# A two-layer language model tower on one core: TensorE multiplies a constant matrix in its waits of the expert stage, and GpSimd's additions for a result are spread over four slots

## The chip, the cores and the metric

The kernel runs on one core of one Trainium2 chip. The core has TensorE (PE, matrix multiply, with its weight loads in a row of their own, PEld), VectorE (DVE), ScalarE (ACT), GpSimd (POOL) and SyncE (SP, which issues DMAs). The metric is the device time of one execution in microseconds (us), lower is better. It is compared as the median of several executions.

## The reference, cut to what matters

16384 tokens of 128 channels go through a token table and four residual layers:

```python
h = tok_table[x]                              # (64, 256, 128)
h = h + linear_attention(layernorm(h))        # first layer
h = h + expert_choice_ffn(layernorm(h))       # 32 experts, each picks its 512 best tokens
h = h + causal_attention(layernorm(h))        # 8 heads of 128, 64 sequences of 256 tokens
h = h + top2_ffn(layernorm(h))                # 8 experts, each token uses 2

# expert_choice_ffn, for expert e: rows idx = its 512 tokens with the highest router probability
up  = tokens[idx] @ W_up[e // 4] + b_up[e // 4]          # 128 -> 341
out = silu(up) @ W_down[e] + b_down[e]                   # 341 -> 128
y[idx] += prob[idx, e] * out
```

All of it is float32.

## The kernel before

The kernel is one program with semaphores placed by hand. The order of instructions on each engine is the order in which the code issues them; no scheduler moves anything. Four stages follow each other: the first layer with the router, the search for each expert's threshold, the **expert stage** (32 experts one after the other), and a long **slot stage** that does the causal attention of 512 sequence-heads in 512 slots (`u` counts them) and, two portions behind, the top-2 feed-forward network.

**The expert stage.** For expert `e` GpSimd issues four indirect DMAs that gather its 4 x 128 token rows into `rows4` (`take(e)`, L836), and later four that scatter the updated rows back (`give(e)`, L845). Its order is `take(e + 1)`, `give(e)`, `take(e + 2)`, `give(e + 1)` and so on. TensorE does per expert, in this order: `rows(e + 2)` (L2000, four matmuls that number the tokens of a later expert), `turn_rows(e)` (L2012, four transposes of the gathered rows into bank 0, behind the wait for the gathers of `e`), then, when ScalarE has copied the transposed rows to `xeT` (L1047), the up product (L2024, three column blocks, with the two small `bases(e + 3)` matmuls L1993 between the second and the third), then, when ScalarE has applied silu (L1059), the down product (L2037, 12 matmuls of fp32, 24 in the profile's count). VectorE counts and places the tokens of later experts, and weighs each down product into `rows4` (L1485), which releases `give(e)`. The gather of `e` must have been issued and landed before `turn_rows(e)`; `give(e)` needs the first L1485 of `e`.

A helper `keep_busy` of the stage before (L1944) already multiplies the constant `slot16` (fp16, 128 x 512) into an unused bank; nothing reads the product. The expert stage has no such multiplications.

**The slot stage.** In slot `u` each engine does a fixed list of things for heads `u`, `u - 1`, ... and, for the feed-forward part, for a unit of 128 token rows. SP loads units; TensorE, ScalarE and VectorE compute one; VectorE ends it with `unit_out` (L1742), and GpSimd scatters it in `give_unit` (L881). In four slots of eight GpSimd also does one `scatter` of normalised rows (L866), and at the first slot of eight `residual` (L875, two additions). From slot 256 on VectorE normalises the softmax (L1567, L1570), and once a slot copies a transposed head out of PSUM (L1577).

When a portion's units are all scattered, results are put together: a table `RESULT_AT` says that in slot `r` SP loads the two expert rows (`zx`, tile name `junk`) and the residual (`h3x`, `pc`) of 512 tokens. GpSimd adds the two rows in slot `r + 2` (`add_rows`, L890, four additions of 128 x 128, behind the wait `z_in` for the loads) and the residual in slot `r + 3` (`add_residual`, L896, four more), and SP stores the result. GpSimd does so for 22 results, those of the first two portions, from slot 386 to 495; consecutive results of a portion are four slots apart. The later ten results are done by VectorE.

Of the kernel before, what the change touches and what calls it, by code (L numbers as in the profile page):

```python
# [12 lines left out]
ALU = mybir.AluOpType  # L13
# [3 lines left out]
P = 128  # L17
C = 128
NTOK = 64 * 256
NT = NTOK // P  # L20
TG = 4
# [67 lines left out]
def lm_tower(nc, x, L0_tok_weight, L0_attn_Wqkv, L0_attn_temperature, L0_attn_Wproj, L0_attn_bproj,  # L89
# [3 lines left out]
    with ExitStack() as ctx:  # L93
# [6 lines left out]
        bank = [ctx.enter_context(nc.psum_tensor(f"bank{n}", [P, 512], F32)) for n in range(8)]  # L100
# [79 lines left out]
        slot16 = sb("slot16", [P, CAP], F16)  # L180
# [140 lines left out]
        zx = junk[:].bitcast(F32).rearrange("p (q j c) -> p q j c", q=2, j=TG)  # L321
# [163 lines left out]
        res_step = sem("res_step")  # L485
# [10 lines left out]
        def gated(i):  # L496
            return 0 <= i < NG
# [237 lines left out]
        def _(pool):  # L735
# [146 lines left out]
                    ap=xu_at(t)[:, C + 1:XW].bitcast(U32), axis=0), in_=yu[:, t % YR], in_offset=None,  # L882
                    bounds_check=2 * NTOK - 1, oob_is_err=False).then_inc(z_out[t % YR], 16)

            def add_rows(c):
                pool.wait_ge(z_in[c % 2], 32 * (c // 2 + 1))
                if c >= 2:
                    pool.wait_ge(out_done[c % 2], 16 * (c // 2))
                for j in range(TG):
                    ins = pool.tensor_tensor(res[:, c % 2, j], zx[:, c % 2, j, 0:C], zx[:, c % 2, j, C:2 * C], ALU.add)  # L890
                ins.then_inc(res_step, 1)

            def add_residual(c):
                pool.wait_ge(res_step, c + 1)
                for j in range(TG):
                    ins = pool.tensor_tensor(res[:, c % 2, j], res[:, c % 2, j], h3x[:, c % 2, j], ALU.add)  # L896
                ins.then_inc(res_ready, 1)

            def normalise(u, h):
                pool.wait_ge(rinv_ready, u + 1)  # L900
                pool.tensor_scalar(pr[:, u % PRN, 0:P], pr[:, u % PRN, 0:P], rinv[:, h % 4, 0:1], None, ALU.mult)  # L901
                pool.tensor_scalar(pr[:, u % PRN, P:3 * P], pr[:, u % PRN, P:3 * P], rinv[:, h % 4, 1:2], None, ALU.mult)\  # L902
                    .then_inc(pr_ready_pool, 1)

            for u in range(NI * 2 * H1):
                n, h = u // H1, u % H1
                i, p = n // 2, n % 2
                if h == 0 and n < NB:
                    residual(n)
                if 0 <= u - N_LAG < POOL_NORM:  # L910
                    normalise(u - N_LAG, (h - N_LAG) % H1)
                if gated(i - 2) and i <= NG and 1 <= h <= TG:
                    if u - 1 <= U:
                        pool.wait_ge(exp_ready, u - 1)
                    scatter(i - 2, p, h - 1)
                if i == NG + 1 and p == 0:
                    scatter(NG - 1, h // TG, h % TG)
                if u - 2 in STEP_AT and STEPS[STEP_AT[u - 2]][2] is not None:
                    give_unit(STEPS[STEP_AT[u - 2]][2])
                if u - 2 in RESULT_AT and u < U:  # L920
                    add_rows(RESULT_AT[u - 2])
                if u - 3 in RESULT_AT and u <= U:
                    add_residual(RESULT_AT[u - 3])
            for q in range(YR):
                pool.wait_ge(z_out[q], given(UNIT0[NK], q))

# [897 lines left out]
        def _(pe):  # L1824
# [179 lines left out]
            for e in range(3):  # L2004
                bases(e)
                if e < 2:
                    rows(e)

            def turn_rows(e):
                pe.wait_ge(xe_in[e % 2], 64 * (e // 2 + 1))  # L2010
                for c in range(TG):
                    ins = pe.transpose(bank[0][:, c * P:(c + 1) * P], rows4[:, e % NTAB, c, 0:C], ident[:])  # L2012
                ins.then_inc(xeT_mm, 1)

            def serve(v, last):
                for q in range(4):
                    e, p = 4 * v + q, q % 2
                    if not (last and q >= 2):
                        rows(e + 2)
                    turn_rows(e)  # L2020
                    pe.wait_ge(xeT_ready, e + 1)
                    pe.wait_ge(wup_in[p], 16 * (2 * v + q // 2 + 1))
                    for k in range(3):
                        pe.matmul(bank[1 + k][0:FCH[k], :], wup[:, p, k * P:k * P + FCH[k]], xeT[:], start=True, stop=True)\  # L2024
                            .then_inc(up_mm, 1)
                        if k == 1 and not (last and q >= 1):
                            bases(e + 3)
                    pe.wait_ge(ac_ready, 3 * e + 3)
                    pe.wait_ge(wdn_in[p], 48 * (2 * v + q // 2 + 1))
                    for c in range(TG):  # L2030
                        if c == 1 and not (last and q >= 1):
                            pe.wait_ge(oneh_ready, e + 4)
                        if TG * e + c >= 2:
                            pe.wait_ge(ye_ready, TG * e + c - 1)
                        for k in range(3):
                            m = FCH[k] + (k == 2)
                            ins = pe.matmul(down_at(c), ac[0:m, k, c * P:(c + 1) * P], wdn[0:m, p, k],  # L2037
                                            start=(k == 0), stop=(k == 2))
                        ins.then_inc(dn_mm, 1)
# [190 lines left out]
```

## Time and profile before

| | |
|---|---|
| median of 3 runs | 2584.89 us (2581.69 to 2586.2) |
| the profiled execution, its own time | 2591.4 us |
| span of the profiled execution | 2589.7 us |
| busy: PE, DVE, ACT, POOL | 2264.2, 1896.1, 1686.8, 1473.5 us |
| mean granted TensorE clock | 0.955 of full speed |

The span is what the records cover; the own time is what the same execution took by the clock that the comparisons use, 1.7 us more. The profiled execution is 6.5 us above the median of the others. Every time at which something starts is counted from the span's start.

### The profile page before, as it was taken

The numbers are of one execution on the slowest core, as the hardware profiler recorded it, in microseconds if no ns is written. First come the engines' busy times: TensorE is split into PE (matmuls) and PEld (weight loads), VectorE is DVE, ScalarE is ACT, GpSimd is POOL, SyncE is SP. The second block draws the span as 40 slices with busy tenths as digits, with TensorE's granted clock in tenths as the row PEclk, the third lists the DMA queues.
The fourth block names the chain that finished last, engine by engine and source line by source line (L and its number), as shares of the span: only waits on it lengthen the run. The fifth ranks groups of instructions, "written<-read, shape, count | busy, mean of one in ns | idle before, by whom it ended". The sixth has DMA issues, their size and how long they took to land.

```text
span 2589.7 us, 59542 instructions
## 1 busy us (share of the span) xinstructions
PE 2264.2 (87%) x16671; PEld 1982.4 (77%) x16687; DVE 1896.1 (73%) x8436; ACT 1686.8 (65%) x5272; POOL 1473.5 (57%) x1870
## 2 busy tenths in 40 slices
PE   4988978576776899999999999999999999999954
PEld 4877756344443788988888899999998888988854
DVE  4877756656663688888888887887788888888622
ACT  3777744122222777777777788888887777777643
POOL 6444200467766578788888864444444665366553
PEclk9999989789888999999999999999999999999987
DMA  2666630244444611111111146566546776476687
GB/s 73 212 229 205 222 121 1 83 138 142 140 135 131 138 42 42 46 45 49 47 44 46 43 135 171 161 163 172 165 134 187 222 217 198 128 227 196 174 254 241
DMA packets 343687, 357.42 MB, mean 138 GB/s; under 512 B 36491, under 2 KB 285931, under 8 KB 343360
## 3 DMA queue, kind: packets, MB, share of 16 engines
q1 hardware_dynamic: 305856, 265.69, 35.9%
q0 software_dynamic: 34048, 80.03, 9.5%
q10 hardware_dynamic: 3456, 7.89, 1.0%
q8 instruction: 138, 2.26, 0.4%
q14 instruction: 189, 1.55, 0.2%
HBM read 211.02 MB, written 136.67 MB: 134 GB/s over the span
## 4 chain that ended last, share of the span: by engine, by line
PE 54%; DVE 22%; DMA 7%; issue 7%; POOL 4%; ACT 3%; SPq 2%; ACTq 0%; DVEq 0%; POOLq 0%
PE bank L2068 6%; PE bank L2158 6%; PE bank L2144 5%; PE bank L2079 4%; PE bank L2024 4%; PE bank L2111 4%; PE bank L2119 3%; PE bank L2067 3%; PE bank L2091 3%; PE bank L2093 3%; PE bank L2092 3%; PE bank L2037 3%; DVE pr_place L1577 2%; DMA rows<-table,idx 2%; DVE nmax L1557 2%
## 5 line engine op out<-in xcount | busy, mean ns | idle before, releaser
L881 POOL DMA_INDIRECT zbuf<-pc,kb x248 | 250.4, 1010 | 272.8 <-DVE pc L1742 221.9
L866 POOL DMA_INDIRECT spread_rows<-kb,pos x256 | 256.1, 1000 | 171.3 <-DVE pc L1742 81.0
L1081 ACT ACTIVATE pr_place<-bank,nmax 128x128 f32<-128x128 f32 x512 | 188.5, 368 | 223.6 <-DVE nmax L1557 223.5
L2068 PE MATMUL bank<-xT,gT 128*128 128x256 f32 x1024 | 307.4, 382 | 0.0
L1577 DVE COPY pr_place<-bank 128x384 f32<-128x384 f32 x512 | 280.6, 548 | 9.2 <-PE bank L2079 7.8
L2158 PE MATMUL bank<-wvo_part,x_part 128*128 128x512 f32 x768 | 269.3, 459 | 0.0
L2079 PE MATMUL bank<-ident,pr_place 128*128 128x128 f32 x1536 | 252.3, 273 | 17.2 <-DVE pr_place L1577 17.0
L1556 DVE TENSOR_REDUCE nmax<-bank 128x1 f32<-128x128 f32 x512 | 142.9, 279 | 169.1 <-PE bank L2068 167.2
L1091 ACT ACTIVATE bank<-causal 128x384 f32<-128x384 f32 x512 | 253.4, 495 | 19.5 <-PE bank L2202 3.3
L2079 PEld LDWEIGHTS bank<-ident,pr_place 128*128 128x128 f32 x1536 | 195.4, 140 | 87.1 <-DVE pr_place L1570 22.1
L2144 PE MATMUL bank<-x_part,wqk_part 128*128 128x256 f32 x1536 | 245.6, 296 | 1.2 <-DVE x_part L1684 1.2
L1083 ACT ACTIVATE pr_place<-bank,nmax 128x256 f32<-128x256 f32 x512 | 242.4, 473 | 0.0
L902 POOL TENSOR_SCALAR pr_place<-pr_place,rinv 128x256 f32<-128x256 f32 x256 | 239.5, 936 | 0.0
L901 POOL TENSOR_SCALAR pr_place<-pr_place,rinv 128x128 f32<-128x128 f32 x256 | 155.4, 607 | 134.4 <-DVE rinv L1563 129.2
L836 POOL DMA_INDIRECT rows<-table,idx x128 | 124.0, 968 | 163.6 <-DVE idx L1470 125.2
L1154 ACT ACTIVATE vo_place<-bank 128x512 f32<-128x512 f32 x256 | 153.1, 598 | 95.8 <-PE bank L2158 95.0
L2091 PE MATMUL bank<-vo_place,pr_place 128*128 128x128 f32 x1024 | 200.6, 278 | 16.8 <-DVE pr_place L1577 15.4
L2067 PE MATMUL bank<-xT,gT 128*128 128x128 f32 x1024 | 203.7, 280 | 10.5 <-ACT gT L1151 10.4
L1557 DVE TENSOR_REDUCE nmax<-bank 128x1 f32<-128x256 f32 x512 | 211.2, 412 | 0.0
L2144 PEld LDWEIGHTS bank<-x_part,wqk_part 128*128 128x128 f32 x1536 | 199.8, 190 | 1.8 <-DVE x_part L1684 1.6
L2093 PE MATMUL bank<-vo_place,pr_place 128*128 128x128 f32 x1024 | 198.6, 276 | 0.0
L2092 PE MATMUL bank<-vo_place,pr_place 128*128 128x128 f32 x1024 | 198.5, 276 | 0.0
(338 smaller groups left out, 6472.9 us busy)
## 6 DMA issues: line engine op xcount, KB each, us to landing
pa<-bundle SPq DMA_DIRECT2D x198, 321.0 KB
table<-rows SPq DMA_DIRECT2D x96, 576.0 KB, 7.0
rows<-table SPq DMA_DIRECT2D x192, 128.0 KB
wu_more<-bundle SPq DMA_DIRECT2D x66, 321.0 KB
junk<-zbuf SPq DMA_DIRECT2D x32, 512.0 KB
kb<-spread_rows SPq DMA_DIRECT2D x248, 65.0 KB
h3buf<-h SPq DMA_DIRECT2D x64, 128.0 KB
kb<-kb SPq DMA_DIRECT2D x32, 256.0 KB
```

Source lines behind the costliest of these rows:

```text
L866: pool.indirect_dma_start(out=spread_rows, out_offset=bass.IndirectOffsetOnAxis(ap=pos[:, k, j:j + 1], axis=0), in_=xr4s[g % 2][:, k, j], ...
L1091: act.activation(bank[SBANK[u % 2]][:, 0:3 * P], causal[:], ACT.Copy).then_inc(mask_set, 1)
L1557: dve.tensor_reduce(nmax[:, h % 4, 1:2], s2[:, P:3 * P], AX.X, ALU.max, negate=True).then_inc(max_ready, 1)
L1577: dve.tensor_copy(prT[:, h % 2], t_bank(u)[:, 0:3 * P]).then_inc(prT_ready, 1)
L2067: pe.matmul(s2[:, 0:P], g[:, 0:P], xT3[:, p, 0:P], start=False, stop=True, skip_group_check=True)
L2068: pe.matmul(s2[:, P:3 * P], g[:, P:2 * P], xT3[:, p], start=False, stop=True, skip_group_check=True)\
L2079: ins = pe.transpose(t_bank(u)[:, k * P:(k + 1) * P], pr[:, u % PRN, k * P:(k + 1) * P], ident[:])
L2091: pe.matmul(o[:, 0:P], prT[:, h % 2, 0:P], v0, start=(h == 0), stop=False, skip_group_check=True)
L2092: pe.matmul(o[:, P:2 * P], prT[:, h % 2, P:2 * P], v0, start=False, stop=False, skip_group_check=True)
L2093: pe.matmul(o[:, P:2 * P], prT[:, h % 2, 2 * P:3 * P], v1, start=False, stop=(h == H1 - 1), skip_group_check=True).then_inc(head_mm, 1)
L2144: ins = pe.matmul(bank[GBANK][:, k * 2 * P:(k + 1) * 2 * P], wqk_part[a][:, h + k], x_part[b][:, p], start=(m == 0), stop=(m == 2))
L2158: ins = pe.matmul(bank[VBANK][:, :], x_part[b][:, p, (h % 2) * P:(h % 2 + 1) * P], wvo_part[a][:, 4 * (h // 2):4 * (h // 2) + 4], start=(m ...
```

## The change

In the expert stage TensorE gets eight more matmuls for each expert: six of `slot16` into bank 0 ahead of the wait for the gathered rows, and two into bank 3 behind the transposes. Both banks are written again by the expert's own work before anything is read from them. In the slot stage GpSimd's eight additions for a result are no longer four in slot `r + 2` and four in slot `r + 3`, but two in each of the slots `r + 2` to `r + 5`: one ahead of the slot's `scatter` and `give_unit`, and one behind them.

```diff
-            def add_rows(c):
-                pool.wait_ge(z_in[c % 2], 32 * (c // 2 + 1))
-                if c >= 2:
-                    pool.wait_ge(out_done[c % 2], 16 * (c // 2))
-                for j in range(TG):
-                    ins = pool.tensor_tensor(res[:, c % 2, j], zx[:, c % 2, j, 0:C], zx[:, c % 2, j, C:2 * C], ALU.add)
-                ins.then_inc(res_step, 1)
+            def add_rows(c, j):
+                if j == 0:
+                    pool.wait_ge(z_in[c % 2], 32 * (c // 2 + 1))
+                    if c >= 2:
+                        pool.wait_ge(out_done[c % 2], 16 * (c // 2))
+                ins = pool.tensor_tensor(res[:, c % 2, j], zx[:, c % 2, j, 0:C], zx[:, c % 2, j, C:2 * C], ALU.add)
+                if j == TG - 1:
+                    ins.then_inc(res_step, 1)
...
+            def adding(u, later):
+                for d in range(2):
+                    if u - 2 - d in RESULT_AT and u - d < U:
+                        add_rows(RESULT_AT[u - 2 - d], 2 * d + later)
+                    if u - 4 - d in RESULT_AT and u - 2 - d < U:
+                        add_residual(RESULT_AT[u - 4 - d], 2 * d + later)
...
+                adding(u, 0)
                 if gated(i - 2) and i <= NG and 1 <= h <= TG:
...
-                if u - 2 in RESULT_AT and u < U:
-                    add_rows(RESULT_AT[u - 2])
-                if u - 3 in RESULT_AT and u <= U:
-                    add_residual(RESULT_AT[u - 3])
+                adding(u, 1)
...
+            def stay_warm(b, times):
+                for _ in range(times):
+                    pe.matmul(bank[b][:, :], slot16[:, 0:P], slot16[:], start=True, stop=True)
+
             def turn_rows(e):
+                stay_warm(0, 6)
                 pe.wait_ge(xe_in[e % 2], 64 * (e // 2 + 1))
...
                     turn_rows(e)
+                    stay_warm(3, 2)
                     pe.wait_ge(xeT_ready, e + 1)
```

(`add_residual` is cut in the same way as `add_rows`.)

TensorE in the expert stage, one expert, before; `oneh` and `tab` belong to the numbering of a later expert, `rows4` holds the gathered rows:

```order
L2000 MATMUL bank5<-tab,oneh 128x129 [waits oneh_ready]
L2000 MATMUL bank5<-tab,oneh 128x129
L2000 MATMUL bank6<-tab,oneh 128x129 x2
L2012 MATMUL bank0<-ident,rows4 128x128 [waits xe_in0]
L2012 MATMUL bank0<-ident,rows4 128x128 x3
L2024 MATMUL bank1<-xeT,wup 128x512 [waits wup_in0,xeT_ready]
L2024 MATMUL bank2<-xeT,wup 128x512
L1993 MATMUL bank7<-cum,before 128x2 [waits cum_ready]
L2024 MATMUL bank3<-xeT,wup 85x512
```

The same place on TensorE after (the lines are those of the changed file: L2012 has become L2024, L2024 has become L2037):

```order
L2007 MATMUL bank5<-tab,oneh 128x129 [waits oneh_ready]
L2007 MATMUL bank5<-tab,oneh 128x129
L2007 MATMUL bank6<-tab,oneh 128x129 x2
L2018 MATMUL bank0<-slot16 128x512 x6
L2024 MATMUL bank0<-ident,rows4 128x128 [waits xe_in1]
L2024 MATMUL bank0<-ident,rows4 128x128 x3
L2018 MATMUL bank3<-slot16 128x512 x2
L2037 MATMUL bank1<-xeT,wup 128x512 [waits wup_in1,xeT_ready]
L2037 MATMUL bank2<-xeT,wup 128x512
L2000 MATMUL bank7<-cum,before 128x2 [waits cum_ready]
L2037 MATMUL bank3<-xeT,wup 85x512
```

Six matmuls stand between the numbering and the wait `xe_in`, and two between the transposes and the wait `xeT_ready`; nothing else has moved.

GpSimd in the slot stage, slots `r + 2` and `r + 3` of the result with `out_done0`, before:

```order
L866 DMA spread_rows<-kb,pos 141312x130 [waits exp_ready]
L881 DMA zbuf<-pc,kb 32768x128 [waits yu_ready]
L890 TENSOR_TENSOR pc<-junk 128x128 [waits out_done0,z_in0]
L890 TENSOR_TENSOR pc<-junk 128x128 x3
L866 DMA spread_rows<-kb,pos 141312x130 [waits exp_ready]
L881 DMA zbuf<-pc,kb 32768x128 [waits yu_ready]
L896 TENSOR_TENSOR pc<-pc 128x128 [waits res_step]
L896 TENSOR_TENSOR pc<-pc 128x128 x3
```

GpSimd from slot `r + 2` to slot `r + 5` of the same result, after (L897 is the old L896):

```order
L890 TENSOR_TENSOR pc<-junk 128x128 [waits out_done0,z_in0]
L866 DMA spread_rows<-kb,pos 141312x130 [waits exp_ready]
L881 DMA zbuf<-pc,kb 32768x128 [waits yu_ready]
L890 TENSOR_TENSOR pc<-junk 128x128 x2
L866 DMA spread_rows<-kb,pos 141312x130 [waits exp_ready]
L881 DMA zbuf<-pc,kb 32768x128 [waits yu_ready]
L890 TENSOR_TENSOR pc<-junk 128x128
L897 TENSOR_TENSOR pc<-pc 128x128 [waits res_step]
L866 DMA spread_rows<-kb,pos 141312x130 [waits exp_ready]
L881 DMA zbuf<-pc,kb 32768x128 [waits yu_ready]
L897 TENSOR_TENSOR pc<-pc 128x128 x2
L881 DMA zbuf<-pc,kb 32768x128 [waits yu_ready]
```

Two runs of four additions have become runs of one or two, with a scatter between them; the wait for the loads (`z_in`) has moved ahead of the scatters of slot `r + 2`, which stood in front of it.

## Rows read from the trace of the kernel before

**Rows 1.** Expert stage: us; PE, PEld, DVE, ACT, POOL busy; PEclk, DMA share, GB/s.

```profile
486.00:828.00 342.00, 249.37 (x1245) 156.86 (x1246) 195.01 (x786) 85.98 (x141) 238.16 (x245) 0.90 0.44 137
```

**Rows 2.** Timeline of GpSimd, expert stage: start, duration, [idle before, releaser].

```profile
488.82 1.01 POOL L845 DMA_INDIRECT table<-rows,idx  x1 [9.84 <-DVE rows L1485]
...
598.86 1.00 POOL L845 DMA_INDIRECT table<-rows,idx  x1 [1.50 <-DVE rows L1485]
...
609.07 1.00 POOL L845 DMA_INDIRECT table<-rows,idx  x1 [0.30 <-DVE rows L1485]
...
633.76 0.99 POOL L845 DMA_INDIRECT table<-rows,idx  x1 [2.18 <-issue]
...
641.40 0.95 POOL L836 DMA_INDIRECT rows<-table,idx  x1 [0.30 <-DVE rows L1485]
...
655.94 1.00 POOL L845 DMA_INDIRECT table<-rows,idx  x1 [3.37 <-DVE rows L1485]
...
817.59 1.00 POOL L845 DMA_INDIRECT table<-rows,idx  x1 [0.30 <-issue]
```

**Rows 3.** Timeline of TensorE, two experts in a row.

```profile
645.34 1.12 PE L2012 MATMUL bank<-ident,rows 128*128 128x128 f32 x4 [4.32 <-DMA rows<-table,idx]
647.14 3.78 PE L2024 MATMUL bank<-xeT,wup 128*128 128x512 f32 x4 [0.69 <-ACT xeT L1047]
...
653.76 3.05 PE L2037 MATMUL bank<-wdn,ac 128*128 128x128 f32 x24 [0.77 <-ACT ac L1059]
656.65 0.39 PE L2000 MATMUL bank<-tab,oneh 128*128 128x129 f16 x4
656.88 0.61 PE L2012 MATMUL bank<-ident,rows 128*128 128x128 f32 x4
658.17 1.98 PE L2024 MATMUL bank<-xeT,wup 128*128 128x512 f32 x4 [0.69 <-ACT xeT L1047]
...
662.45 3.07 PE L2037 MATMUL bank<-wdn,ac 128*128 128x128 f32 x24 [0.77 <-ACT ac L1059]
665.36 0.39 PE L2000 MATMUL bank<-tab,oneh 128*128 128x129 f16 x4
668.25 0.66 PE L2012 MATMUL bank<-ident,rows 128*128 128x128 f32 x4 [2.51 <-DMA rows<-table,idx]
```

**Rows 4.** Single microseconds of the same two experts, the columns of rows 1.

```profile
643.00:644.00 1.00, 0.00 (x0) 0.00 (x0) 0.96 (x4) 0.00 (x0) 0.69 (x2) 0.50 1.06 331
...
658.00:659.00 1.00, 0.83 (x2) 0.49 (x3) 0.97 (x8) 0.30 (x3) 0.70 (x2) 1.00 0.92 267
```

**Rows 5.** Timeline of TensorE in the threshold search: the constant multiplications there.

```profile
359.64 1.02 PE L1944 MATMUL bank<-slot 128*128 128x512 f16 x4
...
362.70 0.59 PE L1944 MATMUL bank<-slot 128*128 128x512 f16 x2
```

**Rows 6.** Line L1577 in two stretches of the slot stage: count, durations, first and last start.

```profile
L1577 DVE COPY pr_place<-bank x96: 536/547/558, 1592.0 to 1923.9; 128x384 f32<-128x384 f32 x96
L1577 DVE COPY pr_place<-bank x49: 536/545/558, 1979.7 to 2164.9; 128x384 f32<-128x384 f32 x49
```

**Rows 7.** Timeline of VectorE and GpSimd at one run of additions.

```profile
2048.96 2.89 DVE L1567 TENSOR_SCALAR pr_place<-pr_place,rinv 128x128 f32<-128x128 f32 x1
...
2049.67 1.70 POOL L896 TENSOR_TENSOR pc<-pc 128x128 f32<-128x128 f32 x4
2051.32 0.86 POOL L875 TENSOR_TENSOR hb<-hx,bo 128x128 f32<-128x128 f32 x2
```

**Rows 8.** Groups by line, VectorE, 1600 to 1900 us, then 1975 to 2165 us.

```profile
L1567 DVE TENSOR_SCALAR pr_place<-pr_place,rinv 128x128 f32<-128x128 f32 x86 | 29.1, 339 | 0.0
...
L1567 DVE TENSOR_SCALAR pr_place<-pr_place,rinv 128x128 f32<-128x128 f32 x49 | 29.3, 598 | 0.0
```

**Rows 9.** Groups by line and shape, GpSimd, 1975 to 2380 us.

```profile
L881 POOL DMA_INDIRECT zbuf<-pc,kb x100 | 101.3, 1013 | 90.0 <-DVE pc L1742 67.9 <-issue 19.3 <-DMA out_dram<-pc 2.7
...
L890 POOL TENSOR_TENSOR pc<-junk 128x128 f32<-128x128 f32 x88 | 38.2, 467 | 28.0 <-DMA pc<-h3buf 27.9
```

More of the change, by code:

```diff
@@ L883, in give_unit, with add_residual @@
                     bounds_check=2 * NTOK - 1, oob_is_err=False).then_inc(z_out[t % YR], 16)
-            def add_rows(c):
-                pool.wait_ge(z_in[c % 2], 32 * (c // 2 + 1))
-                if c >= 2:
-                    pool.wait_ge(out_done[c % 2], 16 * (c // 2))
-                for j in range(TG):
-                    ins = pool.tensor_tensor(res[:, c % 2, j], zx[:, c % 2, j, 0:C], zx[:, c % 2, j, C:2 * C], ALU.add)
-                ins.then_inc(res_step, 1)
[L893 to L897, printed above, removed]
+            def add_rows(c, j):
[6 more added lines that the diff above has]
+                    ins.then_inc(res_step, 1)
+            def add_residual(c, j):
+                if j == 0:
+                    pool.wait_ge(res_step, c + 1)
+                ins = pool.tensor_tensor(res[:, c % 2, j], res[:, c % 2, j], h3x[:, c % 2, j], ALU.add)
+                if j == TG - 1:
+                    ins.then_inc(res_ready, 1)
             def normalise(u, h):
```

## The prediction

> **What bounds the kernel now.** I read the windows of the expert stage first, then the timelines of GpSimd and TensorE in it, then single microseconds of the granted clock, and last, for the additions, the starts of a line that comes once a slot.
>
> In the expert stage no engine looks full: of 342.0 us TensorE is busy 249.37, GpSimd 238.16, VectorE 195.01, and the clock is 0.90 of full speed [rows 1]. GpSimd's 238.16 leaves out the gap of 0.30 us that stands ahead of each of its indirect DMAs. Eight of them per expert, back to back, take 10.21 us (609.07 less 598.86) [rows 2]. That is the least time of an expert. The actual average is (817.59 - 488.82) / 30 = 10.96 us. So over 30 experts GpSimd waits 328.77 - 30 x 10.21 = 22.5 us. One gap of 2.18 us is not for another engine ("issue"): 1.88 us of the 22.5 stay whatever TensorE does.
>
> For the rest the reader is to see two experts in a row on TensorE [rows 3]. The first one's transposes wait 4.32 us for gathered rows and start at 645.34, its down product at 653.76: 8.42 us. The second one starts at 656.88 without a wait and has its down product at 662.45: 5.57 us. The difference of 2.85 us is the clock. TensorE is granted 0.50 at 643 us, after it has stood idle since about 641, so 1.2 GHz instead of 2.4; in the second expert it is at 1.00 [rows 4]. The same up products take 3.78 us in the first and 1.98 in the second. GpSimd pays for it: its first scatter of the slow expert comes at 655.94, 2.18 us after the down product began, and it waited 3.37 us, 3.07 more than the usual 0.30 [rows 2].
>
> In the slot stage a slot lasts (1923.9 - 1592.0) / 95 = 3.49 us where there are no additions for results, and (2164.9 - 1979.7) / 48 = 3.86 us where there are [rows 6]. That is 0.364 us per slot. 22 results times four slots is 88 slots, 32.1 us in all. One instruction shows why: VectorE's L1567, normally 0.339 us in the mean, takes 0.598 in the stretch with additions [rows 8], and one of them takes 2.89 us, until 2051.85, while GpSimd does four additions (from 2049.67) and right behind them the two of L875 (until 2052.18) [rows 7]. VectorE waits for the run, not only for the one addition that it meets.
>
> **The matmuls in the expert stage.** One constant matmul costs TensorE (1.02 - 0.59) / 2 = 0.215 us at full clock [rows 5]. Six are 1.29 us, two are 0.43 us. The two stand in the gap behind the transposes, where TensorE waits 0.69 us for ScalarE's copy [rows 3]: nothing, at full clock. At half clock they are 0.86 us, some 0.2 us too long for that gap. The six stand where the gathered rows are waited for. That wait is 4.32 and 2.51 us at the first experts of two pairs and nothing at the one between [rows 3], which pays the full 1.29 us.
>
> Can TensorE afford it? From one numbering to the next it takes 665.36 - 656.65 = 8.71 us at full clock without a wait for rows. With 1.29 more it is 10.00 us, below GpSimd's 10.21. If GpSimd sets the pace, TensorE waits 10.21 - 10.00 = 0.2 us for rows where it would have waited 1.5. The gaps that remain are 0.2, what is left of 0.69, and 0.77 ahead of the down product, and in the second expert, with gaps of 0.69 and 0.77 us, the clock stayed at 1.00 [rows 3, 4]. The clock should hold.
>
> Is GpSimd then never late? From its last gather of the slow expert (641.40) the transposes could start 3.94 us later, a warm expert needs 5.57 to its down product, and 2.18 more to the first scatter: 11.69 us. GpSimd itself comes to that scatter after the last gather (0.95 + 0.30) and eight more DMAs (10.21), so after 11.46 us. These are 0.2 us too much at worst. Against them stands that in the second expert a small matmul between the up product's blocks (L1993) waits for VectorE's counting; when the up product starts 1.29 us later, VectorE has had that time. I take nothing for it and keep 30 x 0.2 = 6 us as a loss for the range. The first expert starts cold: six matmuls there cost 6 x 0.43 = 2.6 us at most, and nothing if they bring the clock up sooner, which they may, as TensorE no longer pauses; I take nothing. So **20.6 us** (22.5 less 1.88), with ends of 12 (less 6 and 2.6) and 22.5.
>
> The Trainium skill, TensorE: Matmul & The Clock Gate, section "A second HAM failure mode", says that short idle times between groups of matmuls can by themselves make the clock go up and down; the trace speaks against it here (1.00 through gaps of 0.69 and 0.77 us). By it the clock would keep falling, which is the third case below.
>
> **The additions.** Their number stays, 8 x 22 = 176 of 0.467 us [rows 9]; what changes is the length of a run. If VectorE has to wait for what is left of a run of length B, the expected wait per run is B x B / 2 divided by the slot. Before, two results have three runs of 1.70 us and one of 2.51 (with L875) [rows 7]: squares 8.67 + 6.30 = 15.0, over 2 x 3.86 gives 1.94 us, of the 32.1 / 11 = 2.92 us that two results cost. After, a result has two lone additions (0.43 each) and three pairs (0.85), and in every second one L875 (0.86) stands next to a pair: squares 2 x (2 x 0.18 + 3 x 0.72) + 2.2 = 7.2, so 0.94 us. The saving is 1.0 us for two results, **11 us** for 22. The ends are nothing (if only the number of additions counts) and, if the shorter runs lie where VectorE does not need what they hold, most of the 32: I keep 25.
>
> The wait for a result's loads cost GpSimd 28.0 us for 22 results, 1.3 each [rows 9]. It now stands ahead of a scatter of rows and one of a unit, which are no longer done in its shadow: it grows by one or two indirect DMAs, 1.3 to 2.6 us, and they come that much later. Behind them on GpSimd are the next slots' scatters. Who waits: VectorE writes the same of four `yu` buffers again four slots later, 14 us, so two slots are to spare. I take nothing.
>
> **The sum.** 20.6 + 11 = 31.6 us. From the profiled execution's own 2591.4 us that is 2559.8; it stood 6.5 us above the median of the runs shown, so 2553.3, say **2553 us**. The matmuls come first in the program and the additions last, so neither shifts the other's work except as a whole.
>
> **The rivals.** The cases one by one.
>
> Both parts pay as worked out: 2553, with a range of its own of 2545 to 2561. Chance 0.50.
>
> VectorE gets in between any two additions, so that runs do not count, and only the clock pays: 2553 + 11 = 2564. Against it stands the one row of 2.89 us; for it, that the mean of L1567 rose by only 0.26 us. The Trainium skill, SBUF — State Buffer, section "SBUF: two separate sides", has it so: whoever starts first holds the pair for its whole instruction. By it each addition would be a lock of its own. The row shows a wait across several. Chance 0.20.
>
> The clock keeps falling in the expert stage, or TensorE becomes the bound there: a constant matmul at half clock costs 0.43, the six 2.6, and then TensorE's round is 8.71 + 2.6, more than the average 10.96 now. Then the first part brings nothing: 2584.9 - 11 = 2574. Chance 0.09.
>
> The short runs free VectorE nearly wholly (25 us): 2584.9 - 20.6 - 25 = 2539. For it: VectorE's normalisation comes early in a slot, and a pair of additions behind a scatter late. Chance 0.13.
>
> Slower: the wait for loads, ahead of the scatters, is on the path. Each of 22 results then costs the 1.3 to 2.6 us and no shadow: 29 to 57 us, against 20.6 gained and nothing from the runs: 2593 to 2621, say 2600. It decides when a scatter comes over two slots (7 us) late. Against it: waits so far averaged 1.3 us. Chance 0.05.
>
> No difference to speak of, the first expert's loss and short-falls eating a small gain: 2585. Chance 0.03.
>
> **How the numbers follow.** 2553 is the first case. The range of 2540 to 2571 holds it, the second, and about half of the third and fourth; some 2 in 10 are left out. A measurement here tells 0.2%, 5 us, from no change. Faster are the first, second and fourth case and nearly all of the third: 0.91. Same 0.04, slower 0.05.
>
> **What would show it.** The clock of the expert stage near 1.00 instead of 0.90; its 30 experts in about 308 us instead of 328.8; GpSimd's waits for L1485 at 0.3 us nearly everywhere; up products of 1.98 us throughout. In the slot stage, slots with additions at about 3.73 us; no L1567 above 1.8 us. Wrong would be: gaps on TensorE gone but GpSimd as late as before; L1567's mean still near 0.6 us; or GpSimd's idle time for the loads far above 28 us, with VectorE waiting for a scatter behind it.

## The result, and the profile after

The changed kernel takes **2560.38 us** (median of 4 runs, 2558.86 to 2562.14) where the kernel before takes 2585.55 in the same comparison (4 runs, 2581.69 to 2591.54): a ratio of 0.9899 with a 95% interval of 0.9879 to 0.9919, some 25 us less. The profiled execution took 2562.14 us of its own.

The windows of the expert stage, in the columns of [rows 1] and over the same microseconds, and then GpSimd's waits in it by the view of waits (engine, line, releaser, us in all, times, longest):

```profile
486.00:828.00 342.00, 276.51 (x1509) 171.62 (x1509) 204.05 (x822) 88.56 (x147) 245.28 (x250) 0.98 0.48 148
...
POOL table L845 <- DVE rows L1492: 22.7, 29, 10.2
```

The clock is 0.98 where it was 0.90 [rows 1]. The 22.7 us hold the start of the stage (10.2, where it was 9.8 before); the same row of the kernel before read 48.0 us in 45 waits. GpSimd's timeline, first scatter of the first expert and of the one 30 later:

```profile
489.83 1.01 POOL L845 DMA_INDIRECT table<-rows,idx  x1 [10.25 <-DVE rows L1492]
...
799.55 1.00 POOL L845 DMA_INDIRECT table<-rows,idx  x1 [0.30 <-DVE rows L1492]
```

That is 309.72 us for 30 experts instead of 328.77 [rows 2], 3.4 above the floor of 30 x 10.21. TensorE in one expert and at the start of the next (L2007, L2018, L2024, L2037 and L2050 are the numbering, the constant matmuls, the transposes, the up and the down product):

```profile
655.84 0.28 PE L2007 MATMUL bank<-tab,oneh 128*128 128x129 f16 x2
655.95 1.46 PE L2018 MATMUL bank<-slot 128*128 128x512 f16 x6
657.55 0.66 PE L2024 MATMUL bank<-ident,rows 128*128 128x128 f32 x4
658.05 0.59 PE L2018 MATMUL bank<-slot 128*128 128x512 f16 x2
658.90 1.98 PE L2037 MATMUL bank<-xeT,wup 128*128 128x512 f32 x4 [0.26 <-ACT xeT L1054]
...
662.70 3.06 PE L2050 MATMUL bank<-wdn,ac 128*128 128x128 f32 x24 [0.77 <-ACT ac L1066]
665.59 0.39 PE L2007 MATMUL bank<-tab,oneh 128*128 128x129 f16 x4
665.82 1.46 PE L2018 MATMUL bank<-slot 128*128 128x512 f16 x6
668.52 0.66 PE L2024 MATMUL bank<-ident,rows 128*128 128x128 f32 x4 [1.24 <-DMA rows<-table,idx]
```

All products have the length that they have at full clock in [rows 3]; the gaps are 0.26, 0.77 and 1.24 us. In the whole stage the clock fell once, at 637, until 640.25, and again at its end; before, it fell 15 times.

In the slot stage, L1584 (the L1577 of before), for the same slots as in the second row of [rows 6]; then VectorE's L1574 (L1567 before), and GpSimd's first addition, from the groups by line over 1955 to 2145 and 1955 to 2350 us; and the longest hold of the kind in [rows 7]:

```profile
L1584 DVE COPY pr_place<-bank x49: 537/546/556, 1958.6 to 2142.3; 128x384 f32<-128x384 f32 x49
...
L1574 DVE TENSOR_SCALAR pr_place<-pr_place,rinv 128x128 f32<-128x128 f32 x50 | 22.7, 453 | 0.0
...
L890 POOL TENSOR_TENSOR pc<-junk 128x128 f32<-128x128 f32 x87 | 40.8, 486 | 60.1 <-DMA pc<-h3buf 59.6
...
2122.00 0.99 POOL L881 DMA_INDIRECT zbuf<-pc,kb  x1 [1.35 <-DVE pc L1749]
2123.01 0.47 POOL L890 TENSOR_TENSOR pc<-junk 128x128 f32<-128x128 f32 x1
2123.43 0.86 POOL L875 TENSOR_TENSOR hb<-hx,bo 128x128 f32<-128x128 f32 x2
2124.25 0.45 POOL L897 TENSOR_TENSOR pc<-pc 128x128 f32<-128x128 f32 x1
...
2122.71 1.68 DVE L1574 TENSOR_SCALAR pr_place<-pr_place,rinv 128x128 f32<-128x128 f32 x1
```

A slot with additions lasts (2142.3 - 1958.6) / 48 = 3.83 us, 0.03 less than before; in a second profile of the same kernel the same slots last (2133.5 - 1957.0) / 48 = 3.68 us, so one profile tells little of the additions. GpSimd waits 60.1 us for the loads of results where it waited 28.0 [rows 9]. The held instruction, as in [rows 7], is let go 0.14 us after the last addition of the run has begun.

Four of the kernels below ran on chips on which the kernel before takes 2748 and 2752 us instead of about 2585; their times are not set beside the others.

### The profile page after: what moved, and what is told of

Its sections match the earlier page's. It is cut to its first block, busy times and chain, and to the rows that moved or that the text cites. A ratio compares the mean times of both kernels' runs of the same rounds, so it can differ in the third digit from the quotient of the medians.

```text
span 2560.4 us, 60070 instructions
## 1 busy us (share of the span) xinstructions
PE 2283.6 (89%) x16943; PEld 1992.8 (78%) x16943; DVE 1883.7 (74%) x8436; ACT 1687.9 (66%) x5272; POOL 1483.0 (58%) x1870
## 4 chain that ended last, share of the span: by engine, by line
PE 54%; DVE 20%; issue 7%; DMA 7%; POOL 7%; ACT 3%; SPq 2%; DVEq 0%; ACTq 0%; POOLq 0%
PE bank L2081 6%; PE bank L2171 6%; PE bank L2157 5%; PE bank L2092 4%; PE bank L2124 4%; PE bank L2132 4%; PE bank L2080 3%; PE bank L2104 3%; PE bank L2106 3%; PE bank L2105 3%; DVE pr_place L1584 2%; PE bank L2037 2%; DMA rows<-table,idx 2%; PE bank L2050 2%; DVE nmax L1564 2%
## 5 line engine op out<-in xcount | busy, mean ns | idle before, releaser
L1584 DVE COPY pr_place<-bank 128x384 f32<-128x384 f32 x512 | 281.2, 549 | 9.1 <-PE bank L2092 7.7
```

What stands on the lines that cost most here:

```text
L1584: dve.tensor_copy(prT[:, h % 2], t_bank(u)[:, 0:3 * P]).then_inc(prT_ready, 1)
```

## The experiments

**The two parts alone, both together, and more matmuls** (one comparison; the kernel before 2583.82 us in 27 runs). The first has the diff's lines of TensorE and not those of GpSimd, the second the reverse, the third is the changed kernel again, and the fourth is

```diff
-                stay_warm(0, 6)
+                stay_warm(0, 12)
```

Expected of the matmuls alone: 

> The eight constant matmuls per expert alone; the additions as in the kernel before. Theory (the matmuls keep TensorE's clock up and GpSimd's issuing becomes the bound of the expert stage, each part counts for itself): the stage ends 20 us earlier, as in the traces of before and after, where the first L1577 of the slot stage starts 19.6 us earlier. Median 2585 - 20 = 2565, clock of the expert stage near 1.00. Rival (the gain of the whole change comes from the additions, and the profiled execution of before was one with unusually many falls of the clock): 2575 to 2580. Rival (the parts need each other): this one and the additions alone do not sum to 25.

Expected of the additions alone: 

> The spread additions alone, no constant matmuls. Theory (shorter runs of additions hold VectorE up for less): 5 to 9 us less than before, 2576 to 2580; between the traces of before and after the slot stage lost 9.4 us between slot 380 and slot 511, but the medians differ by only 25.2 us, of which the expert stage takes 20, which leaves 5. Rival (the port is held per instruction, runs do not count): 2585, no difference. Rival (the earlier wait for the loads costs): above 2585.

Expected of both again: 

> The changed kernel once more, beside the other runs: 2560, the sum of the two parts alone within 2 us if the parts are independent.

Expected of twelve: 

> The changed kernel with twelve constant matmuls instead of six ahead of the wait for the rows. Theory (TensorE has 10.21 - 10.00 us to spare per expert): TensorE's round becomes 8.71 + 12 x 0.215 = 11.29 us, over GpSimd's 10.21, so TensorE is the bound: 32 experts lose about 1.1 us each, 33 to 35 us more than with six, 2594. Rival (the constant matmuls are free because TensorE waits anyway): 2560, as with six.

Measured: matmuls alone 2567.06 us, ratio 0.9941 (0.9924 to 0.9958); additions alone 2577.07, 0.9976 (0.9961 to 0.999); both 2561.46, 0.9918 (0.9902 to 0.9934); twelve 2578.49, 0.9977 (0.9965 to 0.9988). By medians the parts bring 16.8 and 6.7 us and both 22.4: they add up within the intervals, as they should in stages that follow each other. The interval of the additions alone is wide, 2.6 to 10.1 us. Twelve was expected at 2594.

Twelve is the clean case of TensorE as the bound. Windows of its expert stage, then its timeline over two rounds:

```profile
486.00:815.00 329.00, 296.77 (x1642) 184.28 (x1641) 195.27 (x789) 82.78 (x138) 239.78 (x242) 1.00 0.45 140
...
609.84 2.75 PE L2018 MATMUL bank<-slot 128*128 128x512 f16 x12
...
613.72 1.98 PE L2037 MATMUL bank<-xeT,wup 128*128 128x512 f32 x4 [0.26 <-ACT xeT L1054]
...
617.52 3.06 PE L2050 MATMUL bank<-wdn,ac 128*128 128x128 f32 x24 [0.77 <-ACT ac L1066]
...
620.64 2.75 PE L2018 MATMUL bank<-slot 128*128 128x512 f16 x12
```

The clock is 1.00 and no wait for rows is left, so the round of 620.64 - 609.84 = 10.80 us is TensorE's own. Six matmuls less (1.29 us) make it 9.51 us in the changed kernel, worked out and not measured. The prediction had 10.00.

**The six without the two.**

```diff
                     turn_rows(e)
-                    stay_warm(3, 2)
```

> The two constant matmuls behind the transposes are left out, the six ahead of them stay. If the gap of 0.69 us behind the transposes never mattered to the clock (it was 1.00 through such gaps before), the clock stays at 1.00 and the time at 2561. If the two are needed to hold it, the expert stage falls back towards a clock of 0.90 and the time towards 2577.

2563.42 us, ratio 0.9907 (0.989 to 0.9924); the kernel before 2586.24 in 11 runs, as for the next three. The clock of 486 to 815 us is 0.99, 30 experts take 311.1 us. Without the two behind the transposes the kernel is as fast as these runs can tell.

**All eight additions of a result in one slot**, behind the unit's DMA:

```diff
             def adding(u, later):
-                for d in range(2):
-                    if u - 2 - d in RESULT_AT and u - d < U:
-                        add_rows(RESULT_AT[u - 2 - d], 2 * d + later)
-                    if u - 4 - d in RESULT_AT and u - 2 - d < U:
-                        add_residual(RESULT_AT[u - 4 - d], 2 * d + later)
+                if later and u - 2 in RESULT_AT and u < U:
+                    for j in range(TG):
+                        add_rows(RESULT_AT[u - 2], j)
+                    for j in range(TG):
+                        add_residual(RESULT_AT[u - 2], j)
```

> All eight additions of a result stand in one slot behind the unit's DMA, one run of about 3.4 us; their number and everything else is as in the changed kernel. If the time is set by the length of the runs (squares over two results: 2 x 3.4 x 3.4 = 23, and a little for L875, against 15.0 before and 7.2 after), VectorE loses (23 - 7.2) / (2 x 3.86) = 2.05 us for two results more than in the changed kernel, 22 us in all: about 2583, so about as slow as the kernel before. If only their number counts: 2561.

**2545.81 us**, ratio 0.9839 (0.9819 to 0.9859): better than both kernels, and on the other side of what I expected of long runs. My theory of the additions, that the length of a run is what costs, had this kernel at 2583 and fell here. Two places of its trace, GpSimd and VectorE:

```profile
2051.78 1.74 POOL L890 TENSOR_TENSOR pc<-junk 128x128 f32<-128x128 f32 x4 [0.36 <-DMA pc<-h3buf]
2053.59 1.72 POOL L897 TENSOR_TENSOR pc<-pc 128x128 f32<-128x128 f32 x4
...
2051.65 0.14 DVE L1658 TENSOR_SCALAR dest<-dest 128x8 f32<-128x8 f32 x1
2051.83 0.42 DVE L1660 TENSOR_TENSOR tw<-tw 128x4 f32<-128x4 f32 x1
...
2052.58 0.62 DVE L1749 SCALAR_TENSOR_TENSOR pc<-pa,kb,pc 128x128 f32<-128x128 f32 x1
...
2054.67 0.31 DVE L1574 TENSOR_SCALAR pr_place<-pr_place,rinv 128x128 f32<-128x128 f32 x1
2054.90 0.56 DVE L1577 TENSOR_SCALAR pr_place<-pr_place,rinv 128x256 f32<-128x256 f32 x1
```

During 3.5 us of additions VectorE does instruction after instruction, none late by more than about 0.3 us. The run had waited for its loads (0.36 us) and so did not start right behind a DMA. In [rows 7] and in the hold of 1.68 us above, it did, and the instruction that was held had begun while the DMA was still running.

**An addition between the scatter and the unit's DMA.**

```diff
+                adding(u, 1)
                 if u - 2 in STEP_AT and STEPS[STEP_AT[u - 2]][2] is not None:
                     give_unit(STEPS[STEP_AT[u - 2]][2])
-                adding(u, 1)
```

> The second addition of a slot stands between the scatter and the unit's DMA, so that in slots with a scatter every addition stands alone between two DMAs; the changed kernel has pairs behind the unit's DMA. Run length: pairs (0.85 squared = 0.72 for two) become two lone ones (0.36 for two) in about half of the slots, which is 0.1 to 0.2 us per two results, 1 to 3 us in all: 2558 to 2560. Number alone: 2561.

2565.47 us, ratio 0.9912 (0.989 to 0.9933). Shorter runs still, and no gain; 112 of 133 runs now start right behind a DMA.

**Narrow additions**, 8 columns in place of 128 in every operand of the two lines (`0:8` for `0:C`, `C:C + 8` for `C:2 * C`); the kernel leaves the other 120 columns of the sum out.

> The additions for results take 8 of 128 columns, so they are nearly nothing on GpSimd while all waits, loads and DMAs stay (the output lacks the rest of the sum). It tells what the additions still cost in the changed kernel. My sum leaves 32.1 - 11 = 21 us for them: 2540. If their cost in a slot is something else than VectorE's waits for them (the loads, the multiplications on TensorE for a result, the steps ahead of them), little comes: 2555.

2543.89 us, ratio 0.9831 (0.9811 to 0.9851). So the width of the additions costs the changed kernel 2560.4 - 2543.9 = 16.5 us (from two comparisons), and the version with all in one slot only 2. Its GpSimd waits 76.2 us for the loads of results, from the same place ahead of the scatter:

```profile
L890 POOL TENSOR_TENSOR pc<-junk 128x8 f32<-128x8 f32 x88 | 19.6, 242 | 76.2 <-DMA pc<-h3buf 72.2 <-ACT pr_place L1090 3.3
...
L1584 DVE COPY pr_place<-bank x49: 539/546/556, 1959.4 to 2127.4; 128x384 f32<-128x384 f32 x49
```

The wait itself costs nothing here: the slots last (2127.4 - 1959.4) / 48 = 3.50 us, as without results. With all eight in one slot they last 3.56 (1957.3 to 2128.0), with the matmuls alone 3.84.

**Breaks in GpSimd's row.** The first kernel has the order of before and a break ahead of each run of four: a memset of a spare column, and a wait for it. The second has none ahead, but a wait for the end of each addition before the next one starts, within the runs of four, ahead of L875 and within it. Both have the constant matmuls.

```diff
+            def part():
+                pool.memset(spare[:], 0.0).then_inc(parted, 1)
+                partings[0] += 1
+                pool.wait_ge(parted, partings[0])
...
+                part()
                 for j in range(TG):
                     ins = pool.tensor_tensor(res[:, c % 2, j], zx[:, c % 2, j, 0:C], zx[:, c % 2, j, C:2 * C], ALU.add)
```

The second, where `part(ins)` is a wait for the end of `ins`:

```diff
                 for j in range(TG):
                     ins = pool.tensor_tensor(res[:, c % 2, j], zx[:, c % 2, j, 0:C], zx[:, c % 2, j, C:2 * C], ALU.add)
+                    if j < TG - 1:
+                        part(ins)
```

> Arrangement of the additions as before (four in a slot, four in the next, with the constant matmuls), but ahead of each run of four GpSimd writes one column of a spare tile and waits for it, so that a run no longer starts directly behind an indirect DMA. Theory A (VectorE loses when one of its instructions is under way as a run starts directly behind a DMA, and is then held until the run's last addition): what was held 2.5 to 2.9 us is no longer held, and the time comes to that of all eight in one slot: 2546 to 2550. Theory B (what counts is how many back-to-back additions a run has, wherever it starts): as the same kernel without the breaks, 2567. Theory C (what counts is that every result took two slots): 2567 too.

> Arrangement of the additions as before, with the constant matmuls, but GpSimd waits for the end of each addition before it starts the next one, and also ahead of L875: no run is longer than one addition, and the run still starts directly behind the DMA. Theory A: an instruction of VectorE that is held gets in at the first break, so it loses 0.45 instead of up to 2.9 us: 2548 to 2553. Theory B: the same, 2550. Theory C (two slots per result, not the runs): 2567.

Both fell on chips on which the kernel before takes 2748 us, and the first, repeated, on one where it takes 2752: 

> The same kernel as the one with a wait ahead of each run of four additions. That comparison fell on a chip on which the kernel before takes 2748 us, so its time can't be set beside the others; in its trace hardly an instruction of VectorE is held any more. On a chip on which the kernel before takes about 2585: Theory A (held when under way as a run starts directly behind a DMA) 2546 to 2551; theories B and C (length of the run, or two slots per result) 2567. If a semaphore wait in GpSimd costs more than it saves: over 2567.

Measured: 2781.59 us, ratio 1.0119 (1.0083 to 1.0155); 2783.29, 1.0138 (1.0103 to 1.0173); repeated 2793.4, 1.0138 (1.0102 to 1.0175). None of the times expected came, and as times they decide nothing between the theories: both kernels contain the constant matmuls, and the expert stage has another limit here. TensorE and ScalarE in the expert stage of the first:

```profile
716.38 0.60 PE L2028 MATMUL bank<-ident,rows 128*128 128x128 f32 x4
716.81 0.59 PE L2022 MATMUL bank<-slot 128*128 128x512 f16 x2
723.00 3.78 PE L2041 MATMUL bank<-xeT,wup 128*128 128x512 f32 x4 [5.59 <-issue]
...
722.35 0.60 ACT L1058 ACTIVATE xeT<-bank 128x512 f32<-128x512 f32 x1 [12.80 <-remote]
```

The up product waits 5.59 us, and for ScalarE's copy of the transposed rows (L1058): it starts 0.05 us behind the end of that copy, as in every expert of this kernel and of the kernel before. What is late is the copy. The transposes had ended at 716.98; "remote" means that the profile has no instruction that released ScalarE. In the profile of the kernel before, the copy starts 0.04 to 0.12 us after the transposes in all 32 experts; in the four profiles from these chips it comes over 1 us late in 10 to 14 of them, by 67 to 74 us in sum. 30 experts take 429.27 us here. Why ScalarE starts late stays open, and so does whether the kernel before loses the same there, as no profile of it was taken on such a chip.

The slot stage can be compared within each profile. In the kernel with breaks ahead a slot without additions for results lasts (2108.1 - 1761.6) / 95 = 3.65 us and one with them (2349.2 - 2166.1) / 48 = 3.81, so the additions cost 0.17 us a slot, 0.19 in its repetition and 0.18 with breaks within. With the matmuls alone it is 3.84 less 3.49, 0.35, on a chip where the kernel before takes about 2585. That speaks for the breaks, but is not proof, as a slot without additions is longer here too.

The traces also show what a run of additions does to VectorE, and that needs no comparison of times at all. One place of the first kernel, GpSimd and VectorE:

```profile
2297.58 1.05 POOL L883 DMA_INDIRECT zbuf<-pc,kb  x1 [3.31 <-DVE pc L1753]
2298.76 0.10 POOL L890 MEMSET spare<- 128x1 f32 x1
2298.95 1.90 POOL L900 TENSOR_TENSOR pc<-junk 128x128 f32<-128x128 f32 x4
...
2298.76 0.15 DVE L1231 TENSOR_TENSOR r<-r 128x4 f32<-128x4 f32 x1
2298.83 0.42 DVE L1695 TENSOR_TENSOR x_part<-xT,x_part 128x256 fp32r<-128x256 f32 x1
2299.16 0.55 DVE L1753 SCALAR_TENSOR_TENSOR pc<-pa,kb,pc 128x128 f32<-128x128 f32 x1
```

I counted so in the timelines of seven kernels, over some 400 us of the slots with results each: the runs of additions (gaps between them under 0.03 us), how many of the runs start within 0.05 us of the end of an indirect DMA, and what VectorE's instructions that don't read PSUM lose, in us. The loss is the duration less the one that a fifth of the instructions of the same line and shape stay under; "held" are those that lose over 0.6 us. "Begun before" takes in a few short ones that end up to some 0.2 us ahead of the run.

```
                             runs right behind a DMA:     all other runs:
                       runs  how   begun before   inside    begun before  inside
                             many  n  lost held   n  lost held   n lost    n  lost
before                   45   29   31 38.5  19   39  14.8   7   21  0.2   59   9.1
matmuls alone            46   29   34 36.0  20   31  15.3   7   23  0.1   67   9.1
the changed kernel      120   89  114 31.2  12  106  17.5   4   46  0.6   41   2.5
one between             133  112  164 39.5  19   95  10.9   1   30  0.2   37   3.5
all eight in one slot    57   14   21  7.6   3   13   3.4   1   44  3.2  135  22.1
break ahead              47    2    3  2.1   1    2   0.5   0   51  1.4  166  19.2
breaks within            46   33   45  4.6   0  138  10.5   2   13  0.5   68   6.7
```

At the runs that don't start right behind a DMA none of 801 instructions lost over 0.56 us, however long the run. In the last line four additions count as one run in spite of their breaks, as the rows of the timeline group them.

The sums of the table are no times of VectorE: where two instructions that overlap are held together, both count. They also vary from profile to profile. Counted again over 104 slots, and only for instructions still under way when a run starts right behind a DMA, the losses are 38.4 us before and 34.8 with the matmuls alone, but anything from 20.8 to 36.0 in five kernels with the slot stage of the changed one (itself, its repetition, the additions alone, six and twelve matmuls), then 29.6 with one between, 5.8 with all eight in one slot and 6.9 with narrow additions.

The same count says how firm the rule is. Of the instructions under way when a run of two or more additions starts right behind a DMA, 22 of 26 stay until the last addition has begun in the kernel before, 22 of 24 with the matmuls alone, and 24 of 38 in the changed kernel; at the other runs of two or more it is none of 11, 14 and 2, none of 29 with all eight in one slot and none of 27 with a break ahead. What spares the rest stays open. The count also rules two other readings out. The DMA alone does not hold: an instruction under way at the end of an indirect DMA that no addition follows loses at most 0.27 us in ten profiles (89 of them in the kernel before, none over 0.24). And instructions that read PSUM are not held, even at a run right behind a DMA: none loses over 0.03 us. Each instruction that lost over 0.6 us at such a run had begun while the DMA was running, and ended 0.09 to 0.53 us after the start of the run's last addition.

**All eight at the slot's beginning**, `if not later and ...` in the kernel with all in one slot.

> All eight additions in one slot, at its beginning, ahead of the scatter instead of behind the unit's DMA; the run then stands behind the DMA of the slot before. Theory A: no change in kind, since the first four and the last four still have a wait between them, and a run that has waited for its loads starts behind no DMA: 2546 to 2552. If the good time of the one-slot version is owed to where the additions fall beside VectorE's work, they fall elsewhere now and it is lost: 2560 to 2567.

2832.34 us, ratio 1.0302 (1.0268 to 1.0335), on the chip of 2748 us: by far the worst of the kernels there. Its 131 slots from the 381st on take 521.6 us, where the kernel with breaks ahead takes 479.7. VectorE is hardly held in it: two instructions lose 0.8 and 0.9 us, both at L875. Instead GpSimd waits for loads ahead of the scatter and the unit's DMA, by up to 7.1 us (2150 to 2700 us):

```profile
POOL pc L890 <- DMA pc<-h3buf: 65.9, 18, 7.1
...
ACT pc L1120 <- remote: 39.1, 12, 5.6
```

ScalarE, too, waits for something that no engine shown releases, but does so in all four profiles from these chips. The waits for loads look like my slower rival, a wait for loads on the path of the scatters. That the one causes the other is argued from the order, not shown: the same kernel was not run where the kernel before takes 2585.

## Why the prediction was right, and where it was not

The time of 2560.4 lies in the range; the gain was 25 us instead of 31.6. It lies between the first case (2553) and the second (2564), so the time alone does not tell them apart; the parts alone do.

**The matmuls** are right by their mechanism and nearly by their size; the term was somewhat too large. Forecast: 20.6 us, 30 experts in about 308. In profiles: 309.72 (changed), 308.0 (matmuls alone), 308.35 (both again), 311.1 (six alone), and 308.1 to 312.1 in three more kernels with the six, against 328.77 and 328.39 without them, so 16.3 to 20.8. The medians say 16.8, and the interval of the ratio, 0.9924 to 0.9958, holds 10.9 to 19.6. The case in which the clock keeps falling or TensorE becomes the bound at half clock did not come; twelve matmuls bring the second, at full clock.

Two terms of it were mis-sized and did not matter. TensorE's round is 9.51 us, not 10.00: from the up product to the down product it is 662.70 - 658.90 = 3.80 us, where [rows 3] have 662.45 - 658.17 = 4.28, as the small matmul between the blocks no longer waits for VectorE's counting. I had named this and taken nothing for it; it is worth 0.5 us an expert, more than the 0.2 us that made up the feared loss of 6 us. The first expert is 1.0 us later (489.83 against 488.82), where I had bounds of 0 and 2.6; over the profiles from such chips it lies anywhere from 486.7 to 490.1, so nothing can be read from it. The waits of 0.77, 0.26 and 1.24 us did not bring the clock down, as the prediction read from [rows 3] and [rows 4]. The Trainium skill, TensorE: Matmul & The Clock Gate, section "A second HAM failure mode", would have let it go up and down at such gaps; in this trace it falls once within the stage.

**The additions** brought 5.6 to 6.7 us by medians (2567.06 to 2561.46; 2583.82 to 2577.07), not 11. Their whole cost I had as 32.1 us. From the 381st slot to the last the kernel before takes 475.7 us in its profile and the narrow one 444.0: 31.7. But the profile of before stood 6.5 us above its median; by medians it is 2586.2 - 2543.9 less the 16.8 of the matmuls, 25.5, and the narrow additions are not free. So that term was right or up to a quarter too large. What failed is the step "If VectorE has to wait for what is left of a run of length B, the expected wait per run is B x B / 2 divided by the slot". One run of 1.7 + 1.8 us per result would be the worst by it, and is nearly free. That the change still gained, and over half of the 11 us, is luck: the step that gave the 11 does not hold.

What the runs show in its place, by the table above: an instruction of VectorE that does not read PSUM and is under way when a run of additions starts **right behind an indirect DMA** is in most cases held, and until the run's last addition has begun: 2.89 us in [rows 7], 1.68 after the change. Instructions queued behind the held one are late with it (the 7 "inside" before). At all other runs nothing is held, whatever their length; an instruction begun inside loses 0.1 to 0.2 us in the mean. The change made runs shorter, but three times as many, 89 instead of 29, start right behind a DMA. So the longest hold fell from 2.89 to 1.7 us and the sum only from 38.5 to 31.2, a difference no larger than the one between profiles of the same slot stage. With breaks ahead of the same runs of four it is 2.1, with breaks within them 4.6, and with all eight in one slot 7.6, since there the second four never follow a DMA and most of the first four have waited for loads.

That the holds make the time is argued from three groups of kernels, and not shown step by step. From the 381st slot to the last, the two kernels with the order of before take 475.7 and 471.4 us (38.4 and 34.8 us lost, by the second count), the five with the additions spread 460.1 to 467.7 (20.8 to 36.0), and the two with hardly a hold 446.9 and 444.0 (5.8 and 6.9). Within a group the time does not follow the sum.

For the second case of the prediction, VectorE between any two additions, the runs say: true in runs that do not start behind a DMA, false in the others. The Trainium skill, SBUF — State Buffer, section "SBUF: two separate sides", has one lock that is held for one instruction. The instructions begun inside the other runs fit that (none loses over 0.56 us, little more than one addition); those under way at a start behind a DMA do not: the hold of 1.68 us spans four additions.

**The wait for the loads** grew as forecast in direction, 28.0 to 60.1 us, 1.5 for each of 22 results, in the 1.3 to 2.6 that I had, and cost nothing that these runs can tell: the narrow version waits 76.2 and is the fastest. On the other chips its place may well matter.

Open: what the break ahead of a run would bring in time where the kernel before takes 2585 (the holds say about as much as all eight in one slot); why exactly the DMA matters; what ScalarE waits for on the other chips; and how much of the 1.2 to 1.4% by which both kernels with breaks are slower than the kernel before on the other chips comes from the matmuls, as the matmuls alone were not run there.

## What to carry to other kernels

Before spreading work of one engine to shorten another's waits, look at whether the held instruction was already under way when the run began, and at what the running engine did just before: here it was the DMA ahead of the run, not the run's length, and one long run per result beat four pairs by 15 us. Count the starts of runs, not only their squares.

Constant matmuls in a wait pay while TensorE's round at full clock stays below the pace of the engine that bounds the stage; find how far by doubling them. A version that wins on one chip should be tried on another: the expert stage lost its time elsewhere there.

## What was not expected of the hardware

- An instruction of VectorE that does not read PSUM is in most cases held over a whole run of GpSimd additions (up to 2.61 us above its usual time) if the run starts within 0.05 us of an indirect DMA's end and the instruction is under way then; a memset of one column and a wait for it (0.1 and 0.1 us) between the DMA and the run remove that: 1 hold over 0.6 us instead of 19.
- The same kernel before takes 2585 us on some chips and 2748 to 2752 on others, and 30 experts take 429.27 us in a kernel whose expert stage is the one with 308.0. ScalarE starts its copy of the transposed rows over 1 us late there in 10 to 14 of 32 experts (0.04 to 0.12 us in the profile of the kernel before), and nothing in the profile says what for.
- The clock held at full speed through 12 matmuls of a constant and gaps of 0.26 and 0.77 us for a whole stage (1.00 from 486 to 815 us).
